# Wider gathers in graph attention, next-round loads under a condition, and the mean layer's tile loads split over two blocks

## What is computed

```python
edge_index = jnp.stack([src, dst])
h = relu(layernorm(x)); x = x + L0(h)     # ten steps of degree-weighted propagation
h = relu(layernorm(x)); x = x + L1(h)     # graph attention
h = relu(layernorm(x)); x = x + L2(h)     # dot-product attention with 4 heads
h = relu(layernorm(x)); x = x + L3(h)     # mean of x[src] @ W + b over the edges of a node
# L1: h = x @ W; a_src = h @ att_src; a_dst = h @ att_dst
#     e = leaky_relu(a_src[src] + a_dst[dst], 0.2), then softmax over the edges of dst,
#     out = tanh(segment_sum(h[src] * alpha) + bias)
# L3: out = segment_sum(x[src] @ W + b, dst) / max(in-degree, 1)
```

## Time and profile before

| | us |
|---|---|
| median of three runs | 1673.04 |
| lowest and highest run | 1671.83, 1677.74 |
| the profiled execution | 1673.17 |
| span of its trace | 1671.3 |

### The profile page before, as it was taken

One profiled execution on the slowest core, in us unless ns is written; L12 is line 12 of the kernel. 1 busy time (PEld: TensorE's weight loads), 2 busy tenths in 40 slices (PEclk: granted clock), 3 DMA queues, 4 the chain that ended last, 5 costly groups with the idle time before them and its releaser, 6 DMA issues. The chain is left out here.

```text
span 1671.3 us, 45748 instructions
## 1 busy us (share of the span) xinstructions
PE 1237.1 (74%) x18543; PEld 1166.1 (70%) x18544; DVE 1257.6 (75%) x2253; ACT 550.7 (33%) x1096; POOL 375.4 (22%) x208
## 2 busy tenths in 40 slices
PE   4767777499999999999952037878567777777268
PEld 3356776399999999999952027767557767767268
DVE  7888888555555555555579999999889999999712
ACT  0057777300000000000017743333356666666301
POOL 1400000000000000000000118888525555545200
PEclk6867777699999999999976559898789999999679
DMA  0012222590000000000016745555253334331583
GB/s 10 0 57 106 106 105 98 207 414 6 3 2 3 2 2 3 2 3 2 2 62 194 277 156 199 198 196 200 99 173 140 120 140 140 120 139 61 199 314 105
DMA packets 44602, 182.24 MB, mean 109 GB/s; under 512 B 14627, under 2 KB 16204, under 8 KB 43748
## 3 DMA queue, kind: packets, MB, share of 16 engines
q1 hardware_dynamic: 44052, 177.98, 29.5%
q0 software_dynamic: 336, 1.20, 0.3%
HBM read 135.03 MB, written 44.13 MB: 107 GB/s over the span
## 5 line engine op out<-in xcount | busy, mean ns | idle before, releaser
L1151 PE MATMUL psum<-work,count 128*128 128x192 f16 x6250 | 518.2, 246 | 27.5 <-issue 25.5
L1151 PEld LDWEIGHTS psum<-work,count 128*128 128x128 f16 x6250 | 516.9, 98 | 28.9 <-issue 26.4
L1090 DVE SCALAR_TENSOR_TENSOR work<-psum,small,work 128x96 f32<-128x96 f32 x250 | 79.4, 318 | 228.9 <-PE psum L1151 228.9
L1747 PE MATMUL psum<-count 128*128 128x100 f16 (+1 forms) x1875 | 187.4, 207 | 80.2 <-DVE count L1844 62.2
L1747 PEld LDWEIGHTS psum<-count 128*128 128x128 f16 x1875 | 161.9, 97 | 97.8 <-DVE count L1844 57.3
L1812 POOL TENSOR_TENSOR count<-count 128x1000 bf16<-128x1000 f32 (+1 forms) x75 | 166.7, 2223 | 159.4 <-ACT count L1796 159.4
L1481 PE MATMUL psum<-count 128*128 128x98 f16 x625 | 99.9, 211 | 135.3 <-DVE count L1528 97.8
L928 ACT ACTIVATE work<-work 128x1248 f32<-128x1248 f32 (+1 forms) x6 | 7.2, 1202 | 564.5 <-DVE work L911 564.4
L1520 POOL TENSOR_TENSOR count<-count 128x970 bf16<-128x970 f32 (+1 forms) x75 | 166.6, 2235 | 89.4 <-ACT count L1513 89.4
L1748 PE MATMUL psum<-count 128*128 128x100 f16 (+1 forms) x1875 | 186.4, 207 | 0.0
L1748 PEld LDWEIGHTS psum<-count 128*128 128x128 f16 x1875 | 165.0, 98 | 0.0
(11 more groups left out here) (284 smaller groups left out, 2739.9 us busy)
## 6 DMA issues: line engine op xcount, KB each, us to landing
count<-bucket_rows_by_dst SPq DMA_DIRECT2D x54, 800.0 KB, 4.6
count<-bucket_rows_by_src SPq DMA_DIRECT2D x54, 800.0 KB, 4.2
count_f<-count SPq DMA_DIRECT2D x5, 4000.0 KB, 31.1
count<-count_turned SPq DMA_DIRECT2D x25, 800.0 KB, 5.3
count<-count_f SPq DMA_DIRECT2D x17, 800.0 KB, 4.3
count_turned<-x SPq DMA_DIRECT2D x25, 416.0 KB, 2.4
count_turned<-x SPq DMA_DIRECT2D x25, 384.0 KB, 2.3
work<-count_f SPq DMA_DIRECT2D x8, 800.0 KB, 4.3
```

The costliest lines, as they stand in the source:

```text
L1151: last = nc.tensor.matmul(bank[i % BANKS], count16[:, j, i * P:(i + 1) * P], y[par][:, j, :], start=(j == 0), stop=(j == TILES - 1))
L1747: nc.tensor.matmul(slot(b, i, width), hot[:, t0 + i, :], high[:, of, at:at + width], start=True, stop=False, skip_group_check=True)
```

## The change

Three edits. First, two arrays `wide_high` and `wide_low` of 98 columns for each tile take the place of `bend_high` and `bend_low`. GpSimd fills them with zeros in the layernorm block before graph attention, and `bend_high` and `bend_low` become their last two columns; L1483 and L1484 multiply by all 98 columns and add to all 98 of the slot, zeros to the first 96. Second, `first_loads(nc.sync, k + 1)` and the waits for what it loads stand under `if_one(..., None, ...)`, so that with one round they don't run. Third, `load_first` gets a range: in the layernorm block SP issues tiles 0 to 7, and tiles 8 to 11 are issued at the start of the mean's own block, by the same rule of four in flight.

```diff
@@ graph_attention
-    bend_high, bend_low = (sw.take(2 * TILES, F16).rearrange("p (t n) -> p t n", n=2) for _ in range(2))
+    wide_high, wide_low = (region.take(TILES * GW, F16).rearrange("p (t n) -> p t n", n=GW) for _ in range(2))
+    bend_high, bend_low = wide_high[:, :, D:GW], wide_low[:, :, D:GW]
     def slot_numbers(pool):
+        nc.gpsimd.memset(wide_high, 0.0)
+        nc.gpsimd.memset(wide_low, 0.0)
...
-                            nc.tensor.matmul(ps[:, at + D:at + GW], node_hot[DST][t % 2][:, s, :], bend_high[:, t, :], start=False, stop=False, skip_group_check=True)
-                            last = nc.tensor.matmul(ps[:, at + D:at + GW], node_hot[DST][t % 2][:, s, :], bend_low[:, t, :], start=False, stop=True, skip_group_check=True)
+                            nc.tensor.matmul(ps[:, at:at + GW], node_hot[DST][t % 2][:, s, :], wide_high[:, t, :], start=False, stop=False, skip_group_check=True)
+                            last = nc.tensor.matmul(ps[:, at:at + GW], node_hot[DST][t % 2][:, s, :], wide_low[:, t, :], start=False, stop=True, skip_group_check=True)
@@ graph_attention and dot_attention
         end_round(nc, S.values())
-        first_loads(nc.sync, k + 1)
+        if_one(nc.sync, m, None, lambda: first_loads(nc.sync, k + 1))
     def last_loads_landed(sp):
-        sp.wait_ge(S["cols"], 16)
-        for v in range(2):
-            for p in range(2):
-                sp.wait_ge(S["spread_%d%d" % (v, p)], 16)
+        def landed():
+            sp.wait_ge(S["cols"], 16)
+            for v in range(2):
+                for p in range(2):
+                    sp.wait_ge(S["spread_%d%d" % (v, p)], 16)
+        if_one(sp, m, None, landed)
@@ mean_aggregate
-    def load_first(sp):
-        for t in range(READY):
+    def load_first(sp, t0, t1):
+        for t in range(t0, t1):
             if t >= UNDER_WAY:
                 sp.wait_ge(tile_loaded[t - UNDER_WAY], 16)
             load_turned(sp, t)
-        if_one(sp, m, lambda: load_first(sp))
+        if_one(sp, m, lambda: load_first(sp, 0, 2 * UNDER_WAY))
     def one_loads(sp):
+        load_first(sp, 2 * UNDER_WAY, READY)
         for t in range(READY, TILES):
```

## The result

The kernel after takes 1662.76 us, the median of four runs (1661.65 to 1663.80); beside it the kernel before took 1673.26 us. The ratio is 0.9933, with a 95% interval of 0.9913 to 0.9953. The profiled execution took 1663.21 us, its span is 1661.0. Run again beside the last experiment, the same kernel came to 1663.69 us, ratio 0.9939 (0.9924 to 0.9953).

A forecast was written before the change was run, and what follows sets the result against it. The mean was taken as bound by TensorE, its start waiting for SP's loads, and both attention loops by VectorE. 1673.1 - 12.5 (mean) - 0.5 (graph attention) = 1660.1, said as 1660 us, range 1656 to 1668.

The forecast's parts named there:

- Dead loads: After dot attention: two look-ups replace five unneeded loads and their wait, so W goes out 10.9 us earlier.
- The block's end: Block before the mean: VectorE becomes last instead of SP, so it ends 11.4 us earlier.
- The branch: TensorE's branch into the mean's program: takes 5.0 us instead of 6.2, bounds 3.8 and 6.2.
- Rival A: TensorE's branch before the mean: its instruction fetch queues behind four fresh tile loads; 1666.8 us, chance 0.08.
- The mean: Mean stage: tile loads keep up, so the rest moves as a whole and ends 12.5 us earlier.
- The clock: Graph attention's rounds: with wide gathers TensorE's mean clock rises from 0.92 to 1.00.
- B: Graph attention: TensorE's clock keeps falling and the wide gathers no longer fit; 1671 us, chance 0.10.
- C: Graph attention: TensorE stays at the lower clock and becomes the bound; slower, 1693 us, chance 0.04.
- D: Graph attention: the wide gathers miss their fit by 0.25 us on each tile; 1666 us, chance 0.05.
- These 1.9 us back: Graph attention's rounds away from both ends: VectorE's waits from clock falls vanish, saving 1.9 us.
- The two ends: Start and tail of graph attention's rounds: wide gathers delay VectorE by +1.0 us and +0.4 us.
- The memsets: Layernorm block before graph attention: at most 4.4 us on POOL beside 20 us of VectorE's chain, nothing waits.

The follow-up runs named there:

- the last experiment: Kernel after with narrow gathers, no memsets, and the one-round program ahead of the many-round one; 1655.83 us, ratio 0.9891 to the kernel before.
- e8: Kernel before with only the split of the tile loads, dead loads and their waits kept; 1665.48 us, ratio 0.9935.
- e3: Kernel after without the split, all twelve tile loads issued in the layernorm block again; 1664.51 us, ratio 0.995.
- e2: Kernel before with the padding alone (memsets and 98-column gathers); 1677.71 us, ratio 1.0025.
- e4: Kernel before with only the two arrays and their memsets added, gathers kept narrow; 1676.45 us, ratio 1.0016.
- e6: Kernel after with narrow gathers in the first and last tile and the memsets one block later; 1660.29 us, ratio 0.9905.
- e5: Kernel after with one small VectorE operation added ahead of each one-hot of the sources in graph attention; 1667.61 us, ratio 0.9948.
- e11: Kernel after, unchanged, run again on one chip beside the last experiment; 1663.69 us.
- e9: Kernel after with three more PSUM reductions ahead of each one-hot of the sources in graph attention; 1662.44 us, ratio 0.9919.
- e10: Kernel after with three more PSUM reductions behind each one-hot of the sources in graph attention; 1663.11 us, ratio 0.992.

## Why the prediction came out as it did

It said 1660 us (1656 to 1668) and the time is 1662.8. The sum's gain was 13.0 us, the profiled spans show 10.3. The mechanism at the mean was right; that the number lies so near is in part luck, since terms that were off in both directions partly cancel. Of its signs of being right two did not come: the branch took 3.85 us where 4 to 6 were said, and the waits of L1552 for L1484 sum to 5.2 where 4 or less were said.

- **Dead loads: right.** W goes out 1.8 us after the barrier, where two look-ups at 0.9 were counted, and SyncE's eighth issue is through far ahead of VectorE.
- **The block's end: right, to 0.1 us.** The step "a block ends with the engine that is last, and that is VectorE next" gave 11.4 us, and 11.37 were measured. e8 and e3 show the same step with SyncE last, by 3.4 and by 0.3 us.
- **The branch: the mechanism right, the size off.** The term was 5.0 us, halfway between 3.8 and 6.2; it took 3.85. It meets the near bound though tiles 8 to 11 leave 0.4 us after it has begun. In e3, e8, e2, e4 and before, with four tiles already under way when it begins, it takes 6.1 or 6.2. Loads issued behind it cost nothing, loads ahead of it 2.3 us. Rival A falls with that, and so does my reason for going half way. It was worth 1.2 us more than forecast.
- **The mean: moves as a whole, as said,** and is 0.5 us shorter.
- **The clock: right.** 1.00 in all eight kernels with wide inner gathers. Rivals B and C fall. (Where the prediction says that by the page's rule the time would be the first rival's, B is meant, and it did not come. The 30 us at the lower level were six falls of 5 us on average, not four each.) D also: no reduction waits in the middle in seven of them; in e6 one does, the first, for 1.05 us. This also explains why e6's middle is the shortest: from the 4th to the 10th reduction it takes 16.0 us against 16.6 in the others (e5 apart), since its 4th came late and the one-hots behind these two late reductions took their bare 1.04 us; from the 10th to the 72nd it takes 173.1 us, as in the others.
- **"These 1.9 us back": wrong.** The waits of the middle went (1.86 to 0), and the time did not. The step that failed is the reading of the earlier trace rows: VectorE was busy 185.3 of 187 us, and I took busy for working, so that each wait would be lost time. The one-hots are held 0.5 to 1.1 us by GpSimd's subtraction (1.53 to 2.17 us where the bare one takes 1.04), and the waits lay ahead of the release. The range of durations of that one line was in the trace of before, unread.
- **The two ends: the first too small, the tail with the wrong sign.** +1.0 was forecast for the first gather, and its wait grew by 1.09 (0.72 to 1.81); the second gather's grew by 0.67 more, for which the sum has no term, so that the first four grew by 0.3 to 1.9 over the kernels with wide gathers there (12.0 to 13.5 against 11.7). +0.4 was forecast for the tail, and its two waits grew by 0.57; but the tail got 0.9 us shorter in six of seven kernels with wide gathers there. In the seventh, e11, which is the kernel after again, the tail took 15.2 us at a mean clock of 0.70 (from 1195.2 to 1210.4 us), and in the kernel after 14.2 at 0.90 (1195.5 to 1209.8), so the tail goes with the time at which the clock falls, and that differs between executions of one kernel. With the middle at 0 the rounds give +0.9 in place of -0.5, inside the bounds of -1.9 and +3.9.
- **The memsets: wrong.** The text said that nothing waits for POOL there. Nothing waits on a semaphore; L909 is held without one, for 1.28 us, and 1.1 of them reach the first copy at L1231. The sum had a duration for the memsets (4.4 us, 4.3 measured) and compared it with the wrong thing, VectorE's chain as cover, when VectorE was the victim.
- **The rest** of the gap, 0.8 in the block and 1.0 in dot attention, is the scatter between executions shown above.

Together: 1.2 and 0.5 us more gain at the mean than forecast, 1.4 less in the rounds, 1.1 lost to the memsets, 1.8 of scatter and 0.2 ahead of graph attention's block, which to the rounding makes the 2.7 us between 13.0 and 10.3.

Of the three edits, two carry the gain. The padding did to the clock what it was said to do and costs more than it gives: 1.1 to 1.2 us for the memsets, and rounds of 217.0 to 217.6 us (where no other edit bears on them) against 216.1 to 216.5 with narrow gathers. What stays open is why dot attention takes 320.6 or 321.6 us, and why the medians of e2 and e4 lie further above the kernel before than their profiles account for.

## What to carry to other kernels

Before you count a wait as lost time, look at the spread of durations of the operation behind it: an engine that is busy all the time may be held in part of it, and then a wait ahead of the release is free, as is work put there (6 us of it in e9 and in e10). Ask the same of the engine that holds it: GpSimd's subtraction too was recorded as busy from its start and ended at a nearly fixed distance behind VectorE's one-hot. A block ends with its last engine, so price a cut by what is last next, and ask what the following step meets then, since half of an edit's worth can lie there. A cheap filler on GpSimd is not hidden because nobody waits for it; look at what small operation of VectorE it lands beside.

## What the runs showed of the hardware

- A jump of TensorE's sequencer over a long unrolled program took 3.4 to 3.9 us with no loads ahead of it and 6.1 to 6.2 us with four loads of 800 KB under way. Loads issued 0.4 us after its start did not lengthen it. Behind the work it is hidden.
- A memset of 128x2450 f16 on GpSimd held a 128x25 operation of VectorE for 1.28 us and did not touch the two reductions beside it (1.45 and 1.34 us, as before).
- VectorE's one-hot of 128x3200 takes 1.04 us alone and up to 2.17 beside GpSimd's subtraction, and ends 0.84 to 0.86 us after that ends. The subtraction of 128x970 in turn, begun beside a one-hot, ends 1.76 to 1.90 us after the one-hot, whatever it lasts (2.18 to 2.76 us). Reductions from PSUM of 128x20 were never held (0.16 us).
- With the gathers' 2-column matmuls widened to 98 columns TensorE's clock was granted at 1.00 from 1003 to 1190 us in eight kernels, against 0.92 or 0.93 in six without. TensorE's longest wait for VectorE's product was 1.5 us in both the kernel before and the kernel after.
